# Expert outputs gated on GpSimd and added by accumulating DMAs, in three of four batches

## The reference, cut to what matters

```python
x = x + conv_part(layer_norm(x))      # depthwise 3x3 convolutions, offsets, bilinear sampling, linear attention
t = to_tokens(x)                      # (4, 3136, 96)
masked = top2_of_softmax(ln(t) @ gate_w + gate_b)                    # (b, s, 4), normalised
h = gelu(einsum('bsd,edh->ebsh', ln(t), w1) + b1)                    # 4 experts, 384 hidden units
y = einsum('ebsh,ehd->ebsd', h, w2) + b2
t = t + einsum('bse,ebsd->bsd', masked, y)                           # out = x + sum_e gate_e * (y_e + b2_e)
```

## Time and profile before

| | us |
|---|---|
| median of three runs | 856.83 |
| the profiled execution, its time | 861.11 |
| the profiled execution, its span | 859.3 |
| TensorE busy in the span | 737.2 (86%) |
| VectorE busy | 617.6 (72%) |
| ScalarE busy | 385.6 (45%) |
| GpSimd busy | 328.9 (38%) |

### The profile page before, as it was taken

One profiled execution on the slowest core, in us unless ns is written; L12 is line 12 of the kernel. 1 busy time (PEld: TensorE's weight loads), 2 busy tenths in 40 slices (PEclk: granted clock), 3 DMA queues, 4 the chain that ended last, 5 costly groups with the idle time before them and its releaser, 6 DMA issues.

```text
span 859.3 us, 9579 instructions
## 1 busy us (share of the span) xinstructions
PE 737.2 (86%) x3186; PEld 511.9 (60%) x3186; DVE 617.6 (72%) x1511; ACT 385.6 (45%) x722; POOL 328.9 (38%) x185
## 2 busy tenths in 40 slices
PE   4988998559992999899992999899993997999996
PEld 4656565336761666566761666566661665688885
DVE  5669827797859568798859468899984244477775
ACT  2323222524551316444551316544540136599995
POOL 4002600016659501256659502245586111234443
PEclk9997979679995999999996999999996799999999
DMA  7023100011420100114421100111421000211111
GB/s 177 1 56 127 43 0 1 0 36 56 151 72 18 35 17 25 43 41 113 153 68 26 41 3 25 51 37 52 153 79 43 17 25 17 67 41 57 65 56 33
DMA packets 20258, 45.58 MB, mean 53 GB/s; under 512 B 4977, under 2 KB 9841, under 8 KB 19921
## 3 DMA queue, kind: packets, MB, share of 16 engines
q1 hardware_dynamic: 12480, 30.18, 11.4%
q10 hardware_dynamic: 4656, 9.96, 3.6%
q0 software_dynamic: 3072, 4.82, 2.3%
HBM read 30.30 MB, written 14.65 MB: 52 GB/s over the span
## 4 chain that ended last, share of the span: by engine, by line
PE 59%; DVE 19%; POOL 11%; ACT 4%; issue 4%; DMA 1%; ACTq 1%; POOLq 0%; DVEq 0%
PE py L668 12%; POOL big L1309 11%; PE pd L626 7%; PE ph L525 5%; DVE val L1023 4%; PE pa L477 3%; PE ph L684 3%; PE ph L685 3%; PE ph L686 3%; PE pa L617 2%; PE pd L595 2%; PE py L721 2%; PE ph L706 2%; PE py L718 2%; PE ph L708 2%
## 5 line engine op out<-in xcount | busy, mean ns | idle before, releaser
L1317 POOL TENSOR_TENSOR xbuf<-xbuf,ye 96x448 f32<-96x448 f32 x112 | 206.6, 1845 | 434.7 <-DVE ye L1238 432.8
L668 PE MATMUL py<-hid,w 128*96 128x448 f32 x504 | 238.3, 554 | 16.6 <-DVE ye L1238 8.7
L899 ACT ACTIVATE hid<-ph,b 128x448 f32<-128x448 f32 x252 | 159.0, 634 | 163.7 <-PE ph L686 147.9
L684 PE MATMUL ph<-x_hi,w_hi 96*128 96x448 f32 x252 | 166.1, 659 | 0.0
L1309 POOL DMA_INDIRECT big<-value_table,rows x64 | 113.7, 1776 | 83.4 <-DMA value_table<-valT 64.2
L1238 DVE SCALAR_TENSOR_TENSOR ye<-py,b,gate_all 96x448 f32<-96x448 f32 x112 | 75.3, 675 | 64.9 <-PE py L668 57.3
L668 PEld LDWEIGHTS py<-hid,w 128*96 128x96 f32 x504 | 82.3, 167 | 38.6 <-ACT hid L899 14.2
L685 PE MATMUL ph<-x_lo,w_hi 96*128 96x448 f32 x252 | 94.4, 375 | 0.0
L686 PE MATMUL ph<-x_hi,w_lo 96*128 96x448 f32 x252 | 93.8, 372 | 0.0
L1023 DVE SCALAR_TENSOR_TENSOR val<-xpad,conv_w,val 128x784 f32<-128x784 f32 x80 | 91.2, 1188 | 0.3
L1280 DVE TENSOR_TENSOR hid_lo<-hid,hid_hi 128x448 fp32r<-128x448 f32 x84 | 59.7, 710 | 27.3 <-ACT hid L908 27.2
(11 more groups left out here) (152 smaller groups left out, 1118.2 us busy)
## 6 DMA issues: line engine op xcount, KB each, us to landing
gate_all<-gate_rows SPq DMA_DIRECT2D x56, 336.0 KB
value_table<-valT ACTq DMA_DIRECT2D x8, 1176.0 KB, 7.6
out<-xbuf SPq DMA_DIRECT2D x28, 168.0 KB, 2.1
xbuf<-in_x SPq DMA_DIRECT2D x3, 1176.0 KB, 8.3
big<-value_table,rows POOLq DMA_INDIRECT x64
xbuf<-in_x SPq DMA_DIRECT2D x2, 336.0 KB, 5.1
query<-in_w SPq DMA_DIRECT2D x1, 576.0 KB
w<-in_w SPq DMA_DIRECT2D x1, 576.0 KB
```

The lines of the kernel that those rows point to most:

```text
L668: nc.tensor.matmul(py[e % 2][0:C, 0:GPIX], w2[:, c, :], hid[:, k % 3, :], start=(j == 0), stop=(j == CPE - 1)).then_inc(hid_used, 1)
L684: nc.tensor.matmul(bank, w1_hi[:, cols], xh(b, g), start=True, stop=False)
L899: nc.scalar.activation(hid[:, k % 3, :], ph[k % 2][:, 0:GPIX], ACT.Gelu, bias=b1[:, k % NCH:k % NCH + 1]).then_inc(hid_act, 1)
L1317: ins = p.tensor_tensor(r, r, ye[0:C, e, :], ALU.add)
```

## The change

In batches 0 to 2 ScalarE copies each output with its bias from `py` to `ye`, before the second GELU after the output's last chunk. GpSimd multiplies it by the gate in place and then issues a DMA that adds `ye` to x in SBUF; each such DMA waits until the one before it has landed. ScalarE's copy waits until the addition four outputs back has landed. The indirect DMAs of the gather are dealt out: four (two tiles) at each of outputs 8 to 11, in the last round 6 to 9, between GpSimd's multiplication and its accumulating DMA. VectorE's `turn` calls are gone. Batch 3 keeps VectorE's gating and GpSimd's addition. The chunk numbers of the stages change with it.

```diff
-GATHER_AFTER = 2
+GATHER_AT = 8
+LAST_GATHER_AT = 6
+DEALT = 2
...
-ROUND = [('valT', 28, 3, 19), ('xT', 33, 2, 0), ('keyT', 38, 0, 0), ('pad', 48, 3, 0), ('kv', 54, 0, 42), ('y', 57, 2, 3),
-         ('offT', 61, 0, 0), ('x1c', 64, 3, 24), ('exp', 71, 0, 0), ('gateT', 78, 0, 10.8), ('offc', 80, 0, 0), ('offs', 82, 0, 0),
-         ('tanh', 83, 0, 5), ('end', 84, 0, 4)]
+ROUND = [('valT', 27, 3), ('xT', 33, 3), ('keyT', 38, 1), ('pad', 49, 3), ('kv', 52, 1), ('y', 55, 2),
+         ('offT', 61, 0), ('x1c', 66, 3), ('exp', 75, 0), ('gateT', 78, 0), ('offc', 78, 0), ('offs', 81, 0),
+         ('tanh', 83, 0), ('end', 84, 0)]
-LAST_ROUND = [('valT', 26, 1, 19), ('keyT', 36, 0, 0), ('kv', 54, 0, 33), ('y', 56, 1, 3), ('x1c', 64, 3, 9.6), ('exp', 70, 0, 0),
-         ('gateT', 78, 0, 10), ('end', 84, 0, 1)]
+LAST_ROUND = [('valT', 18, 0), ('keyT', 34, 1), ('kv', 60, 0), ('y', 60, 0), ('x1c', 66, 3), ('exp', 70, 0),
+         ('gateT', 79, 0), ('end', 84, 0)]
...
# SyncE, load_gates and store_result
-                    sp.wait_ge(ye_ready, FREE_OUTPUTS + b * OUTPUTS + EXPERTS * (g - 1) + 2 * k + 2)
+                    gates_used(sp, b * OUTPUTS + EXPERTS * (g - 1) + 2 * k + 2)
-                sp.wait_ge(ye_summed, EXPERTS + b * OUTPUTS + EXPERTS * (g + 1))
+                added(sp, b * OUTPUTS + EXPERTS * (g + 1))
...
# TensorE
-                        pe.wait_ge(ye_ready, FREE_OUTPUTS + b * OUTPUTS + g * EXPERTS + e - 1)
+                        bank_free(pe, b * OUTPUTS + g * EXPERTS + e - 1)
...
# ScalarE, experts
+                def copy_output(n):
+                    g, e = n // EXPERTS, n % EXPERTS
+                    act.wait_ge(hid_used, b * CHUNKS + (n + 1) * CPE)
+                    added(act, b * OUTPUTS + n + 1 - EXPERTS)
+                    nc.scalar.activation(ye[0:C, e, :], py[e % 2][0:C, 0:GPIX], ACT.Identity, bias=b2[:, e:e + 1]).then_inc(out_copied, 1)
                 def gelus_to(end):
                     while done[0] < end:
                         k = done[0]
+                        if k >= CPE + 1 and k % CPE == 1:
+                            copy_output(k // CPE - 1)
...
# VectorE: all turn(...) calls, experts(b) and beside(...) removed; last_experts keeps its gating
-            rest(0, True, no_turn)
-            for b in range(1, BATCH - 1):
-                outputs_to = experts(b - 1)
-                rest(b, True, beside(PLAN, outputs_to))
-                outputs_to(OUTPUTS)
-            outputs_to = experts(BATCH - 2)
-            rest(BATCH - 1, False, beside(LAST_PLAN, outputs_to))
-            outputs_to(OUTPUTS)
+            for b in range(BATCH):
+                rest(b, b + 1 < BATCH)
             last_experts(BATCH - 1)
...
# GpSimd
+            def add_group(b, g, beside):
+                r = x_of(b)[:, g * GPIX:(g + 1) * GPIX]
+                for e in range(EXPERTS):
+                    n = b * OUTPUTS + g * EXPERTS + e
+                    pool.wait_ge(out_copied, n + 1)
+                    if e % 2 == 0:
+                        pool.wait_ge(gate_in[e // 2], 16 * (b * NG + g + 1))
+                    p.tensor_tensor(ye[0:C, e, :], ye[0:C, e, :], gate_all[0:C, e, :], ALU.mult).then_inc(out_gated, 1)
+                    beside(e)
+                    pool.wait_ge(out_gated, n + 1)
+                    wait(pool, out_added, 16 * n)
+                    pool.dma_start(r, ye[0:C, e, :], accum_op=ALU.add).then_inc(out_added, 16)
...
+            for b in range(BATCH - 1):
+                start = GATHER_AT if b < BATCH - 2 else LAST_GATHER_AT
                 for g in range(NG):
-                    sum_group(b, g)
-                    if g == GATHER_AFTER and b < BATCH - 1:
-                        gather(b + 1)
+                    add_group(b, g, lambda e: gather(b + 1, range(NS)[max(0, DEALT * (g * EXPERTS + e - start)):max(0, DEALT * (g * EXPERTS + e - start + 1))]))
+            for g in range(NG):
+                add_last_group(BATCH - 1, g)
```

More of the change, by code:

```diff
@@ L947, in link, with statistics @@
                 need(step(ins))
-            def statistics(np_, nt, eps, with_mean, turn):
+            def statistics(np_, nt, eps, with_mean):
                 S = lambda k: st[0:np_, 0:nt, k]
@@ L979, in bn, with norm_tokens, norm_x @@
                 return last
[L981 removed]
+            def norm_tokens(b, last, back, eps, stats):
                 link(last)
[L984 removed]
+                statistics(TP, NT, eps, False).then_inc(stats, 1)
                 dve.wait_ge(stats, b + 1)
[L986 to L988 removed]
+            def norm_x(b):
                 for g in range(NG):
                     last = bn(b, g, lambda n: tiles_of(n // QUARTERS)[:, :, n % QUARTERS, :], "xT")
[L992 to L993 removed]
+                norm_tokens(b, last, "pad", LN1_EPS, x_stats)
                 by = rstd[0:TP, :].rearrange("p (s o j u) -> p s o j u", j=QUARTERS, o=1, u=1)
@@ L1050, in normalise_off @@
                 link(last)
-                link(statistics(SP, NS, OFF_EPS, True, turn))
-                turn(3.0)
+                link(statistics(SP, NS, OFF_EPS, True))
                 for k in range(NS):
@@ L1112, in head, with rest @@
                 positions(b)
-            def rest(b, with_head, turn):
+            def rest(b, with_head):
                 for k in range(TAPS if first(b) else VALUE_AHEAD, TAPS):
-                    turn(2.7, "valT" if k == TAPS - 1 else None)
                     value_tap(b, k)
@@ L1242, in beside @@
-            def beside(plan, outputs_to):
-                stages = list(plan.dve_us)
-                at, spent = [0], [0.0]
-                def turn(us, name=None, upto=None):
-                    spent[0] += us
-                    if at[0] < len(stages):
-                        this = stages[at[0]]
-                        before = plan.outputs(stages[at[0] - 1]) if at[0] else 0
-                        late = 0 if at[0] else GATES_US
-                        part = min(1.0, max(0.0, spent[0] - late) / max(plan.dve_us[this] - late, 1.0))
-                        number = round(before + (plan.outputs(this) - before) * part)
-                        outputs_to(number if upto is None else min(number, (plan.at(*upto) - 1) // CPE))
-                    if name and name not in plan.dve_us:
-                        outputs_to(plan.needed(name))
-                    elif name:
-                        assert this == name, (this, name)
-                        outputs_to(plan.outputs(name))
-                        at[0] += 1
-                        spent[0] = 0.0
-                return turn
+                            raw_positions(b + 1)
@@ L1302, in _, with gather @@
             p = nc.gpsimd
-            def gather(b):
-                pool.wait_ge(rows_ready, b + 1)
-                pool.wait_ge(table_out, 32 * (b + 1))
-                for k in range(NS):
+            def gather(b, tiles):
+                if 0 in tiles:
+                    pool.wait_ge(rows_ready, b + 1)
+                    pool.wait_ge(table_out, 32 * (b + 1))
+                for k in tiles:
                     for r in range(2):
```

141 lines of the change are left out of this document (49 added, 92 removed).

## The result

The change makes the kernel slower: 871.57 us in the median of four runs (869.63 to 872.62) against 855.94 (854.53 to 860.57) for the kernel before on the same chip, a ratio of 1.017 with a 95% interval of 1.013 to 1.021. The forecast was 885 with a range of 838 to 925. The profiled execution took 869.63 us, its span is 867.8 us. Runs of the kernel before lie mostly in two groups, near 854 us and near 861 us, the second at a lower mean granted clock (0.924 to 0.929 against 0.930 to 0.939), so a ratio can shift by some 0.5% with the share of each.

What follows compares the result with a forecast made beforehand. The prediction named no bound by busy share: TensorE idled some 70 us in three rounds, and GpSimd's SBUF reads starved under VectorE's taps. Rounds of 8 + 8 + 12 = +28 gave 885 us, range 838 to 925 (own range 862 to 910).

Steps and rivals of the forecast that it cites:

- forecast chain: GpSimd's SBUF reads stall under VectorE's strung taps; additions come late, ScalarE's copies wait for them and TensorE stops.
- Query taps sooner: Rounds 1 and 2: query taps begin at 445.1 and end 3 us sooner than before.
- forecast 20: Rounds 1 and 2, under the query taps: TensorE stops 20 us at chunk 43, where before it stopped 16.7 at pad.
- Round 1: Taken to repeat round 2, and to be 8 us slower like it.
- The stop of 8 us in the value taps: Rounds 1 and 2: outputs 1 and 2 are gated late under the taps, so TensorE loses 1.8 + 5.9 = 8 us.
- rival 1: GpSimd gets a turn between taps everywhere, so no stop in the value taps; together -38, 819 us; chance 0.13.
- forecast +5.1: Rounds 1 and 2: kv products at about 489.5 against 484.4 before, with two chunks fewer done by then.
- Round 3: TensorE stands 24 us at chunk 22, kv comes at 685 against 661.6; +12 us for the round.
- 8.2 + 5.5 - 2.5: Round 3 around kv: 8.2 for six chunks, 5.5 for the slow clock after idleness, 2.5 given back by the new stop.
- Landing: Accumulating DMA lands 3.0 us after its issue starts, so the chain needs 3.1 us an output against TensorE's 4.1.
- that contention: Accumulating DMAs carry 84 x 168 KB = 14 MB over DMA engines busy for 19%, which was to cost nothing.
- Direct DMA issue: GpSimd's direct DMA issues do not stall behind taps: taken as 0, with +12 if they stall as indirect ones do.

Runs made afterwards that it cites:

- e1: Changed kernel with query taps 2 to 8 of rounds 1 to 3 run block by block, each tap waiting for the one before; 845.18 us, 0.988.
- e2: Changed kernel with a one-byte-per-partition memset behind every third query-tap instruction in rounds 1 to 3; 844.49 us, 0.988.
- e10: Changed kernel with one memset of one byte per partition, only behind the first query tap of batches 1 to 3; 843.49 us, 0.982.
- e5: Kernel before the change with a one-byte memset behind every third query-tap instruction; 853.2 us, 1.002.
- e6: Changed kernel with the stage numbers of the kernel before put back; 871.05 us, 1.012.
- e12: Changed kernel with one memset behind the first query tap and another behind key tap 1; 842.95 us, 0.981.
- e11: Changed kernel with one memset of one byte per partition ahead of the first query tap of batches 1 to 3; 840.60 us, 0.979.
- e8: Changed kernel with the tiles val and query allocated in the opposite order; 869.22 us in a single run.
- e3: Changed kernel with GpSimd adding the gated output to x itself instead of by accumulating DMA; 889.06 us, 1.041.

## Why the prediction was right, and where it was off

**Direction and mechanism: right.** Each link of the forecast chain is in the trace: GpSimd's read held under the query taps for 20 to 22 us, the missing addition, the copy, the stop of TensorE in the second layer instead of at `pad`. e1, e2 and e10 change only the order of the query taps or what stands between them, take the starvation away and give some 25 to 30 us back.

**Query taps sooner: right.** They began at 434.41 - 362.1 = 72.3 us into round 2, against 448.25 - 368.8 = 79.4 before; the forecast had 3 us, it was 7, as the forecast stop in the value taps did not come. That shortens the way to kv, and pays part of the stop of 21.14 us (forecast 20).

**Round 1: +1.5 instead of +8.** The mis-sized term. The prediction read round 2 closely and wrote that round 1 repeats it, though the earlier trace rows have no row of round 1. It does not repeat it: the kernel before has one more stop in round 1, where TensorE waits for VectorE's first output under the value taps (TensorE's timeline of before):

```profile
190.05 1.78 PE L668 MATMUL py<-hid,w 128*96 128x448 f32 x2 [8.30 <-DVE ye L1238]
```

The change takes that wait of 8.30 us away, as VectorE has no output to gate. A stop of 6.92 us for the value taps stands in the trace of after in its place, as the taps took 22.8 us; beside it stand 21.28 us for the 16.68 of before.

**The stop of 8 us in the value taps: wrong.** It was to come of multiplications held there. Multiplications of 1.15 to 1.73 us got in under the 18 value taps of every round, and the taps were longer for it (20.7 to 22.8 us; at 0.95 each, 17.1). There rival 1 (GpSimd gets in) was right; under query and key taps the forecast was. The prediction had one such row of before, 397.96, and set it down as an exception. More rows of before would not have settled it: under its strings of three value taps additions took 1.76 us in some (387.89) and 3.69 in others (404.89), to the end of the taps. And the first six value taps of a round, ahead of `positions`, were closed in rounds 1 and 3 of after and open in round 2 (GpSimd's timeline):

```profile
174.89 5.30 POOL L1261 TENSOR_TENSOR ye<-ye,gate_all 96x448 f32<-96x448 f32 x1
...
365.76 1.44 POOL L1261 TENSOR_TENSOR ye<-ye,gate_all 96x448 f32<-96x448 f32 x1 [2.21 <-ACT ye L897]
```

Round 2 came to +8.8 for the forecast +8 all the same. That is luck in part: the stop in the value taps (forecast 8 us) was missing, and the kv products came no sooner for it; what took the difference is not shown. The stops were 21.14 + 2.02 us for 16.7, and the kv products were done 124.5 us into the round for 118.4, which is +6.1 for the forecast +5.1, with two chunks fewer done by then.

**Round 3: +7.0 instead of +12.** kv was forecast at 685, which is 125.6 us into the round, and came at 124.8 (686.3 less 561.5). The stop was smaller, 6.00 + 10.24 us instead of 24, as the multiplication waited from 606 and not from 589: those ahead of it got in under the value taps. What came back behind kv was larger: 69.8 us were left of the round for 85.4, so 15.6 where the forecast had 11.2 (8.2 + 5.5 - 2.5). The sixteen products ran in 5.32 us together where the last eight alone had taken 5.41, and the granted clock in the last stretch was 1.00 against 0.90.

**Landing: 3.5 us instead of 3.0, and two that were late.** In the chain of waits of after the landings at 430.97 and 458.18 took 3.54 and 3.45 us. Additions of the kernel after that wait only for each other follow at 3.9 us (issues at 185.04, 188.94, 192.82 and 196.70), forecast 3.1. That is under TensorE's 4.1 us an output, so it costs nothing. In round 2 two additions had 9.3 and 10.0 us from their issue to the next (389.06 to 398.39, 411.68 to 421.66): the first beside the load of batch 3's x, the second beside the write of the value table, each 1176 KB. The prediction had priced that contention at nothing; TensorE did not stop for it there.

**Direct DMA issue: right at 0.** 84 issues took 804 to 993 ns, those under closed strings too (0.95 us at 173.80, 0.99 us at 240.67). (The Trainium skill, "SBUF — State Buffer", section "Who interferes with whom", says that VectorE's two-input instructions contend with GpSimd's instructions that read SBUF and not with those that only write; the trace agrees, as far as the DMA issue counts among the latter.)

**Against the rule taken word by word.** The Trainium skill, "SBUF — State Buffer", section "SBUF: two separate sides", has whoever starts first keep the shared ports for its whole instruction, and the prediction weighed that against the 21.55 us of the earlier trace rows. The runs bear out the row in closed strings (a read held for 19.90 us under some 20 taps, not for one) and the rule in open ones.

**The sum.** 8 + 8 + 12 = +28 forecast, 1.5 + 8.8 + 7.0 = +17.3 by the trace, less 0.6 in the last experts; +15.6 by the medians. The actual time lies inside the forecast's own range of 862 to 910, and the direction and the stop that carries it were forecast; the single terms were hit less well, and the errors of rounds 1 and 3 have the same sign.

**Not settled.** What makes a string open or closed. Open were the 18 value taps of all rounds (with the tiles swapped too), the block-by-block taps, and the query taps of the changed kernel with a memset at their start. Closed were its query taps otherwise, most key taps, and the query taps of e5 in rounds 1 and 2 in spite of seven memsets. Both states were met in the first six value taps of a round and in key taps (e6, e12), under the same instructions, so the instructions alone don't decide. In round 2 of e12 the same memset did let a waiting gather issue in (3.01 us), so the kind of the waiting instruction is not the answer for e5.

## What to carry to other kernels

An engine's share of busy time says little about whether work can be put on it: GpSimd was busy for 38% before, but its SBUF reads could stand still for 20 us, and the change put a chain with four slots behind them. When work moves to GpSimd, look for the strings of two-input VectorE instructions beside it, count the slots between its output and the engine that sets the pace, and try a tiny instruction of another kind at the start of such a string before giving the idea up: here that turned 1.7% slower into some 2% faster (1.3 to 3.0% in e11). It is a thing to measure and not to count on: in e5, and in the key taps of e12 in rounds 1 and 3, such an instruction did nothing. And read every repetition of a loop for stops, not one for all: the largest error of the forecast in a round's sum was a stop that only round 1 had.

## What the runs showed of the hardware that was not expected

- A string of two-input VectorE instructions can be closed or open to GpSimd's SBUF reads, mostly for all of its length (in round 2 of e6 it changed on the way). Closed, it held one for up to 22.54 us (e8, from the last key taps to the end of the query taps); open, gather issues take 1.5 to 1.6 us instead of 0.97, multiplications mostly 1.4 to 1.6, and single taps up to 2.97 us instead of 1.02.
- One memset of 128 bytes (60 ns) at the start of the query taps opened them in e10 and e11, in three rounds of three. In e5 seven of them did not, in rounds 1 and 2, and in the key taps of e12 one did in round 2 alone.
- A second SBUF read per output by GpSimd made 18 value taps last 29.55 us instead of 20.68 (e3 against the kernel after, round 2).
- An accumulating DMA of 168 KB inside SBUF took 3.5 us from issue to landing; beside a transfer of 1176 KB the next one could be issued 9.3 and 10.0 us after it. The value table's own landing went from 7.6 us to 9.0 in the median.
